# Attention and quantised FFN in one kernel: key rows split over ScalarE and GpSimd, weight maxima earlier, quantising moved around

## The chip, the cores and the metric

The kernel runs on one core of a Trainium2 chip. The metric is the device time of one execution in microseconds (us). Three runs of the kernel before gave 394.27, 394.17 and 396.25; their median is 394.27 us.

## What is computed

Eight sequences of 512 tokens with 512 channels pass through one gated cross-attention block and one gated feed-forward block. The attention is over channels, not tokens: in each of 4 heads a 128 x 128 score matrix is built from 512 tokens, once with a set of global weights and once with local ones. The feed-forward block quantises its inputs and weights to integers with one scale for a whole tensor, so that a maximum over everything has to be known before the first product.

```python
def _channel_attention(qm, km, vm, scale):            # 4 heads
    scores = einsum('bhdn,bhen->bhde', qh, kh) * scale
    attn = softmax(scores, axis=-1)
    return einsum('bhde,bhen->bhdn', attn, vh)
att = attention(q*wqg+bqg, k*wkg+bkg, v*wvg+bvg) + attention(q*wql+bql, k*wkl+bkl, v*wvl+bvl)
x = x + tanh(g_xattn) * (2.0 * att * wp + bp)         # q = layernorm(x), k = v = ctx
def _qlinear(x2d, w, b):
    xq, sx = x/scale rounded, scale = max(max|x|, 1e-6)/127      # one scale per tensor
    wq, sw = the same of w
    return (xq @ wq.T + b) * (sw * sx)
x = x + tanh(g_ffn) * _qlinear(gelu(_qlinear(layernorm(x), w1, b1)), w2, b2)   # 512 -> 2048 -> 512
```

## The kernel before, in words

There is no scheduler: each engine's program is written out by hand, and semaphores join them. Three stages follow each other.

**Attention, steps b = -1 to 7.** A step works on two batches: it finishes batch b and begins batch b+1. Step by step, in the order in which TensorE takes them:
- `gram(b+1)` (L917): products of normalised queries and keys, four heads, 16 matmuls of 129 columns.
- `turn_weights(b)` (L948): transposes of the normalised exponentials. ScalarE's `weights_out` (L433) copies them out of PSUM.
- `key_sums(b+1)` (L925) and `turn_columns` (L930): small products that give the bias terms of the scores.
- `constant_sums(b)` (L958).
- `rank_terms(b+1)` (L937): the bias terms of the scores as a product of two narrow tiles. Its left side is `L_sb` (ScalarE, L440), its right side are the **key rows** `Rh`: (psK + a column) times a constant tile, on 64 partitions (VectorE, `key_rows`, L586).
- `value_product(b)`: a constant row (L969, it needs VectorE's `constant_row`, L650) and the product with the transposed context (L975, it needs `value_weights`, L657).

VectorE's order in step b (2 to 5): `statistics(b+2)` (L556, L560), `columns` (L568), `products` (L577, two), one piece of `w1_max` (L615), `largest_square(b-1)` (L600), `key_rows(b+1)` (L586), `constant_row(b)` (L650), `value_weights(b)` (L657), `scores(b+1)` (L594, eight), `add_product(b)` (L664, four), with `reciprocals` (L635) ahead of its last tile. ScalarE: `weights_out`, `left_rows`, `local_out` (L446), `normalise(b+2)` (L454), `exponentials(b+1)` (L463), `squares(b)` (L425). GpSimd: `rstd_x(b+2)` (L322 to L327), `key_sum(b+2)` (L334, L337), `rstd_out(b-1)` (L351, L357), `weighted(b+1)` (L342, L345: exponentials times their reciprocal sums).

Beside this the first weight matrix is loaded in four quarters `load_w1(0..3)` (L237), each with a semaphore of its own (`w1_in0` to `w1_in3`). `w1_max` reduces it in 16 pieces, four to a quarter. Before, pieces 0 to 3 are taken in step 0, 4 to 8 in steps 1 to 5, 9 to 15 in step 6, where the scale of w1 is made (L694 to L624, with a transpose on TensorE, L907). GpSimd then quantises w1 in eight pieces (L364 and L366 each): five in step 6, three in step 7, and each releases a load of w2. In step 6 VectorE, not GpSimd, weights batch 7's exponentials (L643). The loads of SyncE are issued in the order of its program; `load_k(b)` waits for `gram(b-2)`, `load_cT(b)` for `value_product(b-2)`.

**The scale of x.** After the last attention step VectorE forms the largest normalised value: L727, L732, L735, L737, a transpose on TensorE, L740; GpSimd takes the root (L388), after its own last `rstd_out` (L357); VectorE makes the scale and its reciprocal (L743 to L749) and quantises batch 0 tile by tile (L771, L766), TensorE transposes each tile (L1031), VectorE copies them (L787).

**The two products of the feed-forward block** (L1069 with gelu on ScalarE, L513; L1100 with L851). Hidden values of five batches are spilled to memory and read back.

## Time and profile before

| | |
|---|---|
| median of 3 runs | 394.27 us (394.17 to 396.25) |
| the profiled execution | 394.15 us, its span 392.3 us |
| PE (TensorE matmul) busy | 365.2 us, 93% |
| DVE (VectorE) busy | 320.3 us, 82% |
| ACT (ScalarE) busy | 259.2 us, 66% |
| POOL (GpSimd) busy | 105.5 us, 27% |
| chain that ended last, by engine | PE 80%, DVE 13%, issue 3%, DMA 2%, ACT 1%, POOL 1% |
| attention, from the first product L917 to the last L975 | 13.9 to 143.4 us |
| first FFN product L1069, second L1100 | from 155.0, from 277.7 us |

Times in the profile count from the span's start. The busy shares are averages over stages with different limits. The chain of waits goes back from the last instruction to what released each piece of work; a piece's time in it is only what lies on the chain. A granted clock of 1.00 is TensorE at 2.4 GHz, 0.50 is 1.2 GHz. PEld is TensorE's weight load, SPq the queue of SyncE.

### The profile page before, as it was taken

How to read it: one execution, taken by the hardware profiler on the slowest of the kernel's cores; microseconds unless marked ns; L12 is line 12 of the kernel's file. 1: busy time of each engine (PE TensorE's matmuls, PEld its weight loads, DVE VectorE, ACT ScalarE, POOL GpSimd, SP SyncE). 2: the span in 40 equal slices, each digit the busy share in tenths (PEclk: the TensorE clock that was granted, in tenths of full speed). 3: DMA queues.
4: the chain of work that ended last, by engine and by line, in shares of the span. 5: the costliest groups of instructions: out<-in, count | busy, mean ns of one | idle time of the engine just before them, and what ended most of it. 6: DMA issues, size and time to landing. Idle time of an engine off the chain costs nothing.

```text
span 392.3 us, 5890 instructions
## 1 busy us (share of the span) xinstructions
PE 365.2 (93%) x2087; PEld 218.0 (56%) x2110; DVE 320.3 (82%) x599; ACT 259.2 (66%) x474; POOL 105.5 (27%) x169
## 2 busy tenths in 40 slices
PE   6779899999997797999999999999999999999995
PEld 4657787687685675454455455455544444444442
DVE  3289999999999877999999989978598876686653
ACT  1578877877874450789959988788899997620000
POOL 2653855855845661039200000000000000000000
PEclk9699999999999698999999999999999999999999
DMA  7999987843232550467767760000499999920123
GB/s 223 321 376 382 388 304 281 270 176 100 100 109 67 201 162 3 186 254 297 301 248 305 304 250 0 3 0 2 179 390 402 424 427 423 340 119 28 81 109 107
DMA packets 14528, 84.74 MB, mean 216 GB/s; under 512 B 1889, under 2 KB 2145, under 8 KB 5026
## 3 DMA queue, kind: packets, MB, share of 16 engines
q1 hardware_dynamic: 13840, 83.89, 56.3%
q10 hardware_dynamic: 658, 0.46, 0.5%
q8 instruction: 17, 0.28, 0.3%
q14 instruction: 13, 0.11, 0.1%
HBM read 54.99 MB, written 29.36 MB: 215 GB/s over the span
## 4 chain that ended last, share of the span: by engine, by line
PE 80%; DVE 13%; issue 3%; DMA 2%; ACT 1%; POOL 1%; DVEq 0%; SPq 0%; POOLq 0%
PE PS L1069 28%; PE PS L1100 28%; PE PS L975 7%; PE PS L917 7%; DVE mxd L600 3%; PE PS L937 2%; PE PS L969 2%; PE PS L1031 2%; DVE mid L577 2%; DMA X<-in_x 2%; DVE ring L643 1%; PE PS L958 1%; DVE mid L586 1%; DVE hmax L615 1%; PE PS L948 1%
## 5 line engine op out<-in xcount | busy, mean ns | idle before, releaser
L513 ACT ACTIVATE ring<-PS,bias,sc 128x512 f32<-128x512 f32 x128 | 97.1, 782 | 30.3 <-PE PS L1069 17.3
L1069 PE MATMUL PS<-mid,w1q 128*128 128x512 bf16 x500 | 111.9, 382 | 1.8 <-DVE mid L787 1.3
L1100 PE MATMUL PS<-w2q,w1q 128*128 128x512 bf16 x501 | 110.0, 379 | 1.1 <-DVE w1q L869 0.6
L1100 PEld LDWEIGHTS PS<-w2q,w1q 128*128 128x128 bf16 x512 | 49.9, 98 | 60.9 <-issue 0.5
L1069 PEld LDWEIGHTS PS<-mid,w1q 128*128 128x128 bf16 x512 | 50.0, 98 | 60.7 <-issue 2.6
L800 DVE TENSOR_REDUCE hmax<-ring 128x1 f32<-128x2048 f32 x30 | 67.5, 2278 | 5.4 <-ACT ring L513 5.4
L532 ACT ACTIVATE ring<-ring,sc 128x2048 f32<-128x2048 f32 x30 | 57.6, 1990 | 7.2 <-DMA ring<-spilled_hidden 7.2
L860 DVE TENSOR_SCALAR w1q<-ring 128x2048 bf16<-128x2048 f32 x30 | 36.6, 1223 | 22.8 <-PE PS L1100 18.7
L917 PE MATMUL PS<-ring 128*128 128x129 f32 x256 | 32.0, 286 | 1.4 <-ACT ring L454 1.4
L975 PEld LDWEIGHTS PS<-w2q,ring 128*128 128x128 f32 x256 | 29.2, 192 | 6.1 <-issue 6.1
L917 PEld LDWEIGHTS PS<-ring 128*128 128x128 f32 x256 | 31.2, 202 | 1.7 <-issue 1.7
L975 PE MATMUL PS<-w2q,ring 128*128 128x128 f32 x256 | 30.7, 278 | 0.0
L463 ACT ACTIVATE ring<-mid,nb 128x128 f32<-128x128 f32 x64 | 24.7, 388 | 8.3 <-DVE nb L594 8.3
L556 DVE BATCH_NORM_STATS2 st<-X 128x6 f32<-128x512 f32 x32 | 19.9, 681 | 11.9 <-issue 6.1
L851 DVE SCALAR_TENSOR_TENSOR X<-PS,sc,X 128x512 f32<-128x512 f32 (+1 forms) x33 | 22.9, 730 | 8.1 <-PE PS L1100 7.1
L664 DVE SCALAR_TENSOR_TENSOR X<-PS,X 128x512 f32<-128x512 f32 x32 | 21.8, 688 | 4.8 <-PE PS L975 4.4
L454 ACT ACTIVATE ring<-X,nmr,rstd 128x512 f32<-128x512 f32 x32 | 23.4, 811 | 3.2 <-POOL nmr L327 3.2
L903 PE MATMUL PS<-ident 128*128 128x128 f32 x124 | 19.7, 314 | 5.3 <-POOL ident L310 3.5
L425 ACT ACTIVATE ring<-X,nmean 128x512 f32<-128x512 f32 x32 | 22.8, 714 | 0.5
L903 PEld LDWEIGHTS PS<-ident 128*128 128x128 f32 x124 | 17.7, 221 | 8.0 <-POOL ident L310 3.5
L879 DVE TENSOR_TENSOR X<-X,mid 128x1024 f32<-128x1024 f32 x16 | 19.4, 1218 | 0.0
L337 POOL TENSOR_TENSOR mid<-mid,ring 128x512 f32<-128x512 f32 x16 | 18.9, 1184 | 1.3
(108 smaller groups left out, 405.6 us busy)
## 6 DMA issues: line engine op xcount, KB each, us to landing
spilled_hidden<-ring SPq DMA_DIRECT2D x20, 1024.0 KB, 3.9
ring<-spilled_hidden SPq DMA_DIRECT2D x20, 1024.0 KB, 8.9
ring<-in_ctx SPq DMA_DIRECT2D x8, 1024.0 KB, 10.0
ring<-in_ctxT SPq DMA_DIRECT2D x8, 1024.0 KB, 5.3
X<-in_x SPq DMA_DIRECT2D x7, 1024.0 KB, 12.8
out<-X SPq DMA_DIRECT2D x7, 1024.0 KB, 10.5
ring<-in_w1T SPq DMA_DIRECT2D x4, 1024.0 KB, 10.4
ring<-in_w2T SPq DMA_DIRECT2D x8, 512.0 KB, 3.8
```

The costliest lines, as they stand in the source:

```text
L454: nc.scalar.activation(q_sb[b % 2][:, i].rearrange("p h d -> p (h d)"), X[:, b, i, :], ACT.Identity, scale=rstd1[:, i:i + 1], bias=nmr1[:, ...
L463: nc.scalar.activation(E_sb[:, j, :], S_sb[:, j, :], ACT.Exp, scale=-1.0, bias=nb[:, j:j + 1], accum_out=Z[:, j:j + 1]).then_inc(exp_done, 1)
L513: nc.scalar.activation(ring[:, s * CH + c, (h % CH) * N:(h % CH + 1) * N], PS[:, hidden_bank(s, h), :], ACT.Gelu, scale=S1, bias=bias1[:, ...
L532: nc.scalar.activation(r, r, ACT.Copy, scale=ISH, bias=MAGIC).then_inc(hy_done, KH // CH)
L800: V.tensor_reduce(hmax[:, bass.ds(CH * g + c, 1)], ring[:, s * CH + c, :], AX.X, ALU.max, apply_absolute_value=True).then_inc(hm_done, 1)
L851: V.scalar_tensor_tensor(xi, PS[:, par * NT + i, a:a + n], S2, xi, ALU.mult, ALU.add).then_inc(out_done, 1)
L860: V.tensor_scalar(hq[:, c].rearrange("p k n -> p (k n)"), ring[:, s * CH + c, :], MAGIC, None, ALU.subtract).then_inc(hq_done, KH // CH)
L903: nc.tensor.matmul(PS[:, bank, 0:P], ident[:, :], ident[:, :], start=True, stop=True)
L917: mm = nc.tensor.matmul(psG[:, h // 2, h % 2, :], q_sb[b % 2][:, i, h, :], k_sb[b % 2][:, i, h, :], start=(i == 0), stop=(i == NT - 1))
L975: mm = nc.tensor.matmul(PS[:, OUT_BANK[i], h * P:(h + 1) * P], cT_sb[b % 2][:, h, i, :], M_sb[b % 2][:, h, :], start=False, stop=(h == NH ...
L1069: mm = nc.tensor.matmul(PS[:, hidden_bank(s, h), :], w1v[:, k, h * P:(h + 1) * P], xqT[:, s, k, :], start=(k == 0), stop=(k == NH - 1))
L1100: mm = nc.tensor.matmul(PS[:, par * NT + i, :], hq[:, c, k, i * P:(i + 1) * P], w2v[:, kk, :], start=(kk == 0), stop=(kk == KH - 1))
```

## The change

- **Key rows** of batches 2 to 7: ScalarE copies psK out of PSUM with the column added (`key_copy`, behind `weights_out`), and GpSimd multiplies by the constant tile (`key_rows`, behind `rstd_x`). Batches 0 and 1 stay on VectorE.
- **Weight maxima**: pieces 0 to 2 before step -1, 3 in step -1, 4 to 7 in step 0, b+7 in step b (1 to 5), 13 to 15 in step 6. `load_w1(0)` and `load_w1(1)` are issued three loads earlier.
- **GpSimd** quantises pieces 0 and 1 of w1, then waits until batch 7's exponentials are weighted (`en_done`), and then does pieces 2 to 4 (and 5 to 7 as before).
- **The scale of x**: the root gives the inverse at once, so one reciprocal and one product leave the path; they and the bias go to `x_scale`, behind the first quantising.
- **Batch 0's quantising**: tiles 1 and 3 are scaled by ScalarE, 0 and 2 by VectorE.
- **Warm-up matmuls** before the first product: 11 where there were 2.

```diff
@@ -247,14 +248,14 @@
...
             load_x(1)
+            load_w1(0)
             load_k(1)
...
             load_cT(0)
-            load_w1(0)
+            load_w1(1)
             load_k(2)
...
             load_cT(1)
-            load_w1(1)
             for b in range(2, B):
@@ -305,7 +306,6 @@
...
                 nc.gpsimd.memset(k_sb[s][:, :, :, P:HEAD], 1.0).then_inc(consts, 1)
-            nc.gpsimd.memset(PHALF, 0.5)
             pool.wait_ge(zeroed, 3)
@@ -335,6 +335,11 @@
...
+            def key_rows(b):
+                pool.wait_ge(kc_done, b - 1)
+                nc.gpsimd.tensor_tensor(Rh[0:64, :], Rh[0:64, :], rowc[0:64, :], ALU.mult).then_inc(rh_done, 1)
@@ -369,11 +374,17 @@
...
                     rstd_x(b + 2)
+                if 1 <= b < B - 1:
+                    key_rows(b + 1)
+                if b + 2 < B:
                     key_sum(b + 2)
-                if b >= 1 and b < B:
+                if 1 <= b < B:
                     rstd_out(b - 1)
                 if b == B - 2:
-                    for q in range(5):
+                    quantise_w1(0)
+                    quantise_w1(1)
+                    pool.wait_ge(en_done, 8 * B)
+                    for q in range(2, 5):
                         quantise_w1(q)
@@ -385,7 +396,7 @@
...
             pool.wait_ge(xs_step, 4)
-            nc.gpsimd.tensor_tensor(XROOT, XALL, PHALF, ALU.pow).then_inc(xs_pow, 1)
+            nc.gpsimd.tensor_tensor(XROOT, XALL, half[:, 0:1], ALU.pow).then_inc(xs_pow, 1)
@@ -432,6 +443,12 @@
...
+            def key_copy(b):
+                act.wait_ge(sk_done, b + 1)
+                act.wait_ge(r_done, b)
+                nc.scalar.activation(Rh[0:64, :], psK, ACT.Identity, scale=1.0, bias=acol[0:64, 64:65]).then_inc(kc_done, 1)
@@ -480,6 +497,8 @@
...
                 weights_out(b)
+                if 1 <= b < B - 1:
+                    key_copy(b + 1)
                 if b + 1 < B:
@@ -496,6 +515,10 @@
...
             act.wait_ge(t_done, B)
+            act.wait_ge(xs_step, 7)
+            for i in (1, 3):
+                nc.scalar.activation(ring[:, 3, i * D:(i + 1) * D], X[:, 0, i, :], ACT.Identity,
+                                     scale=rstd[:, i:i + 1], bias=nmr1[:, i:i + 1]).then_inc(ya_done, 1)
             act.wait_ge(scales, 1)
@@ -677,27 +700,29 @@
...
             statistics(1)
+            w1_max(range(0, 3))
             dve.wait_ge(blocks_in, 32)
...
                 if b == B - 2:
-                    w1_max(range(9, 13))
+                    w1_max(range(13, 16))
                 if b + 1 < B:
...
                 if 1 <= b < B - 2:
-                    w1_max([b + 3])
+                    w1_max([b + 7])
                 if b == B - 2:
-                    w1_max(range(13, 16))
                     dve.wait_ge(w1_step, 4 * NH)
...
                     largest_square(b - 1)
-                if b + 1 < B:
-                    key_rows(b + 1)
+                if b == -1:
+                    key_rows(0)
+                    w1_max([3])
                 if b == 0:
-                    w1_max(range(0, 2))
+                    key_rows(1)
+                    w1_max(range(4, 6))
                 if b == B - 2:
@@ -715,7 +740,7 @@
...
                 if b == 0:
-                    w1_max(range(2, 4))
+                    w1_max(range(6, 8))
                 if b >= 0:
@@ -740,14 +765,19 @@
...
             dve.wait_ge(rstd_done, B)
-            V.tensor_scalar(SX, XROOT, MIN_RANGE, 1.0 / QP, ALU.max, ALU.mult).then_inc(xs_step, 1)
+            V.tensor_scalar(ISX, XROOT, QP, QP / MIN_RANGE, ALU.mult, ALU.min).then_inc(xs_step, 1)
             dve.wait_ge(xs_step, 5)
-            V.reciprocal(ISX, SX).then_inc(xs_step, 1)
-            V.tensor_tensor(S1, SX, SW1, ALU.mult).then_inc(xs_step, 1)
-            dve.wait_ge(xs_step, 7)
             V.tensor_scalar(rstd[:, :], rstd[:, :], ISX, None, ALU.mult).then_inc(xs_step, 1)
-            V.tensor_scalar(bias1[:, :], B1, S1, None, ALU.mult).then_inc(scales, 1)
+            dve.wait_ge(xs_step, 6)
+            V.tensor_tensor(nmr1[:, :], nmean[:, 0:NT], rstd[:, 0:NT], ALU.mult).then_inc(xs_step, 1)
+            def x_scale():
+                V.reciprocal(SX, ISX).then_inc(xs_step, 1)
+                dve.wait_ge(xs_step, 8)
+                V.tensor_tensor(S1, SX, SW1, ALU.mult).then_inc(xs_step, 1)
+                dve.wait_ge(xs_step, 9)
+                V.tensor_scalar(bias1[:, :], B1, S1, None, ALU.mult).then_inc(scales, 1)
@@ -758,24 +788,32 @@
...
                     dve.wait_ge(hm_done, CH * (g - SLOTS + 1) + 1)
-                dve.wait_ge(xs_step, 8)
+                dve.wait_ge(xs_step, 6)
                 yt = ring[:, s * CH + 3, :].rearrange("p (i d) -> p i d", i=NT)
                 xq = ring[:, s * CH + 2, 0:CW // 2].bitcast(BF16)
+                first = isinstance(g, int) and g == 0
+                def normal(i, inc):
+                    V.tensor_scalar(yt[:, i, :], X[:, g, i, :],
+                                    nmean[:, bass.ds(4 * g + i, 1)], rstd[:, bass.ds(4 * g + i, 1)],
+                                    ALU.add, ALU.mult).then_inc(y_done, inc)
                 def to_integers(i):
-                    dve.wait_ge(y_done, 4 * g + i + 1)
+                    if i % 2 == 0:
+                        dve.wait_ge(y_done, i + 2)
+                    else:
+                        dve.wait_ge(ya_done, (i + 1) // 2)
                     V.tensor_scalar(xq[:, i * D:(i + 1) * D], yt[:, i, :], MAGIC, MAGIC, ALU.add,
...
-                first = isinstance(g, int) and g == 0
-                for i in range(NT):
-                    V.tensor_scalar(yt[:, i, :], X[:, g, i, :],
-                                    nmean[:, bass.ds(4 * g + i, 1)], rstd[:, bass.ds(4 * g + i, 1)],
-                                    ALU.add, ALU.mult).then_inc(y_done, 1)
-                    if first and i > 0:
-                        to_integers(i - 1)
                 if first:
-                    to_integers(NT - 1)
+                    normal(0, 2)
+                    normal(2, 2)
+                    for i in range(NT):
+                        to_integers(i)
                 else:
+                    for i in range(NT):
+                        normal(i, 1)
                     dve.wait_ge(y_done, 4 * g + 4)
@@ -801,6 +839,7 @@
...
             quantise_x(0, 0, 0)
+            x_scale()
             evacuate(0, 0)
@@ -983,10 +1022,12 @@
...
             mm.then_inc(spread_done, 1)
+            keep_warm(2, 6)
             pe.wait_ge(nmr_done, 1)
-            keep_warm(1, 6)
-            pe.wait_ge(q_done, 1)
-            keep_warm(1, 6)
+            keep_warm(3, 6)
+            for i in range(NT - 1):
+                pe.wait_ge(q_done, i + 1)
+                keep_warm(2, 6)
             pe.wait_ge(consts, 9)
@@ -1046,7 +1087,7 @@
...
             keep_warm(4)
-            pe.wait_ge(xs_step, 8)
+            pe.wait_ge(xs_step, 6)
             keep_warm(3)
...
             pe.wait_ge(w1q_done, PIECES)
```

**VectorE, step 1.** Before (the left name is the tile written, `hmax` holds the maxima, `mxd` the largest squares; `w1_in1` and `w1_in2` are the semaphores of w1's second and third quarter):

```order
L568 TENSOR_TENSOR acol<-PS,colv 128x2x4 [waits aT_done,g_done]
L577 TENSOR_TENSOR mid<-PS,w2q 128x512 [waits exp_done]
L577 TENSOR_TENSOR mid<-PS,w2q 128x512
L615 TENSOR_REDUCE hmax<-ring 128x1 [waits w1_in1]
L600 TENSOR_REDUCE mxd<-ring 128x4 [waits sq_done]
L586 SCALAR_TENSOR_TENSOR mid<-PS,acol,mid 64x512 [waits r_done,sk_done]
L650 TENSOR_TENSOR ring<-PS,mid 128x512 [waits o_done,c_done,scaled]
```

Now:

```order
L591 TENSOR_TENSOR acol<-PS,colv 128x2x4 [waits aT_done,g_done]
L600 TENSOR_TENSOR mid<-PS,w2q 128x512 [waits exp_done]
L600 TENSOR_TENSOR mid<-PS,w2q 128x512
L638 TENSOR_REDUCE hmax<-ring 128x1 [waits w1_in2]
L623 TENSOR_REDUCE mxd<-ring 128x4 [waits sq_done]
L673 TENSOR_TENSOR ring<-PS,mid 128x512 [waits o_done,c_done,scaled]
```

The key rows have left VectorE's queue, and the maximum in it waits for another quarter of w1.

**SyncE, the first loads.** Before, and then now (`in_ctx` are the keys, `in_ctxT` the transposed context):

```order
L228 DMA ring<-in_ctx 128x16x128
L222 DMA X<-in_x 128x2048
L228 DMA ring<-in_ctx 128x16x128
L222 DMA X<-in_x 128x2048
L234 DMA ring<-in_ctxT 128x2048
L237 DMA ring<-in_w1T 128x2048
L228 DMA ring<-in_ctx 128x16x128 [waits g_done,ks_step]
L222 DMA X<-in_x 128x2048
L234 DMA ring<-in_ctxT 128x2048
L237 DMA ring<-in_w1T 128x2048
L228 DMA ring<-in_ctx 128x16x128 [waits g_done,ks_step]
```

```order
L229 DMA ring<-in_ctx 128x16x128
L223 DMA X<-in_x 128x2048
L238 DMA ring<-in_w1T 128x2048
L229 DMA ring<-in_ctx 128x16x128
L223 DMA X<-in_x 128x2048
L235 DMA ring<-in_ctxT 128x2048
L238 DMA ring<-in_w1T 128x2048
L229 DMA ring<-in_ctx 128x16x128 [waits g_done,ks_step]
L223 DMA X<-in_x 128x2048
L235 DMA ring<-in_ctxT 128x2048
L229 DMA ring<-in_ctx 128x16x128 [waits g_done,ks_step]
```

The first and the second quarter of w1 stand three loads earlier; behind the last row the order is the same in both, with the third quarter three loads on.

**GpSimd, step 6.** Now (`sc` holds the scale of w1; before, five pairs like the first stood here with no wait on `en_done`, and no row `kc_done`):

```order
L342 TENSOR_TENSOR mid<-mid 64x512 [waits kc_done]
L356 TENSOR_SCALAR ve<-ssq 128x4 [waits sq_done]
L362 TENSOR_TENSOR rstd<-ve,half 128x4 [waits ve_done]
L369 TENSOR_SCALAR ring<-ring,sc 128x1024 [waits w1_step]
L371 TENSOR_SCALAR w1q<-ring 128x1024 [waits w1y_done]
L369 TENSOR_SCALAR ring<-ring,sc 128x1024 [waits w1_step]
L371 TENSOR_SCALAR w1q<-ring 128x1024 [waits w1y_done]
L369 TENSOR_SCALAR ring<-ring,sc 128x1024 [waits w1_step,en_done]
L371 TENSOR_SCALAR w1q<-ring 128x1024 [waits w1y_done]
```

The third pair now waits until batch 7's exponentials are weighted.

## Rows read from the trace of the kernel before

**Rows 1.** Chain of waits, step 2: start, us on the chain, what

```profile
57.30 0.17 DVE acol L568
...
58.66 0.59 DVE hmax L615
59.26 2.16 DVE mxd L600
61.41 0.70 DVE mid L586
...
62.25 1.09 PE PS L937 x3
...
71.61 0.17 DVE acol L568
```

**Rows 2.** Timeline, step 2: start, us, engine, line, operation, tiles, count

```profile
58.07 1.07 PE L925 MATMUL PS<-mid,ring 128*64 128x512 f32 x2
58.18 1.09 ACT L433 ACTIVATE w2q<-PS 128x512 f32<-128x512 f32 x2 [0.46 <-PE PS L948]
...
59.31 2.05 PE L958 MATMUL PS<-w2q 128*128 128x128 f32 x16
```

**Rows 3.** Groups by line and shape: busy us, mean ns, idle before

```profile
L454 ACT ACTIVATE ring<-X,nmr,rstd 128x512 f32<-128x512 f32 x32 | 23.4, 811 | 3.2 <-POOL nmr L327 3.2
...
L337 POOL TENSOR_TENSOR mid<-mid,ring 128x512 f32<-128x512 f32 x16 | 18.9, 1184 | 1.3
```

**Rows 4.** One line (L237) in the window 39 to 40 us: third quarter of w1

```profile
L237 SPq DMA_DIRECT2D ring<-in_w1T x1: 433/433/433, 39.4 to 39.4; - x1
...
DMA to landing us min/median/max: 10.2/10.2/10.2
```

**Rows 5.** Windows: length, busy of PE, PEld, DVE, ACT, POOL, clock, DMA share, GB/s

```profile
14.00:35.00 21.00, 18.96 (x114) 13.83 (x114) 15.95 (x57) 14.39 (x43) 12.44 (x16) 0.91 1.01 378
35.00:49.00 14.00, 12.88 (x105) 10.96 (x103) 14.00 (x46) 11.84 (x37) 8.35 (x17) 1.00 1.01 372
```

**Rows 6.** Timeline, step 1, VectorE

```profile
44.27 0.67 DVE L615 TENSOR_REDUCE hmax<-ring 128x1 f32<-128x512 f32 x1
...
47.72 0.67 DVE L650 TENSOR_TENSOR ring<-PS,mid 128x512 f32<-128x512 f32 x1
```

**Rows 7.** Windows around the two late low stretches of the clock

```profile
136.50:140.00 3.50, 2.66 (x18) 1.71 (x17) 1.28 (x2) 0.00 (x0) 3.42 (x4) 0.86 0.01 2
...
156.80:160.00 3.20, 3.20 (x14) 1.33 (x13) 3.09 (x3) 2.26 (x4) 0.00 (x0) 0.82 0.00 0
```

**Rows 8.** Chain of waits, from step 6 to the first FFN product

```profile
122.05 1.14 PE PS L969 x8
...
127.16 4.79 DVE ring L643 x8
...
137.79 0.70 DVE ring L650
...
146.55 0.09 DVE ve L727
...
148.69 0.56 POOL sc L388
...
152.20 0.46 DVE ring L771
...
155.03 8.29 PE PS L1069 x31
```

**Rows 9.** Timeline of the fill, VectorE

```profile
15.17 2.47 DVE L556 BATCH_NORM_STATS2 st<-X 128x6 f32<-128x512 f32 x4 [6.09 <-issue]
...
27.87 1.67 DVE L643 TENSOR_SCALAR ring<-ring,rw 128x128 f32<-128x128 f32 x8
```

**Rows 10.** Timeline, GpSimd, the first two of eight pieces of w1

```profile
121.41 1.13 POOL L364 TENSOR_SCALAR ring<-ring,sc 128x1024 f32<-128x1024 f32 x1 [5.08 <-DVE sc L624]
...
123.65 1.13 POOL L364 TENSOR_SCALAR ring<-ring,sc 128x1024 f32<-128x1024 f32 x1
```

More of the change, by code:

```diff
@@ L85, in gated_xattn_ffn @@
         (W1MAX, W1ALL, SW1, ISW1, W2MAX, W2ALL, SW2, ISW2, XMAX, XALL, XROOT, SX, ISX, S1,
-         HMAX, HALL, SH, ISH, S2, PHALF) = (sc[:, i:i + 1] for i in range(20))
+         HMAX, HALL, SH, ISH, S2) = (sc[:, i:i + 1] for i in range(19))
         w1max, w2max4 = hmax[:, 0:4 * NH], hmax[:, 4 * NH:4 * NH + CH]
@@ L170, in gated_xattn_ffn @@
             ("q_done", "ks_step", "g_done", "sk_done", "rh_done"))
+        kc_done, ya_done = sem("kc_done"), sem("ya_done")
         a_done, aT_done, L_done, r_done = (sem(n) for n in ("a_done", "aT_done", "L_done", "r_done"))
```

## The prediction

> **What bounds the kernel now.** I read the page first: TensorE is busy 93% of the span and the chain that ended last is TensorE for 80%, so a gain has to come from where TensorE waits. Then the chain of waits in order of time. The two 8-batch matmul phases behind 155 us (L1069, L1100) run without gaps that the diff touches, so they are left as they are. What the diff touches lies in the first 155 us, and there the chain leaves TensorE once per attention step. The reader is to see this in [rows 1], step b=2: one piece of weight maximum (0.59), the largest square (2.16) and the key rows (0.70) stand in VectorE's queue one behind the other, and only then do the rank terms L937 run, at 62.25. TensorE had ended its last work, L958, at 59.31+2.05=61.36 [rows 2]. A step lasts 71.61-57.30=14.31 us, and the chain repeats these rows for b=2 to 5.
>
> **Steps 2 to 5: the key rows leave VectorE.** The key sums L925 end at 58.07+1.07=59.14, and ScalarE's weights_out L433 at 58.18+1.09=59.27 [rows 2]. The new key_copy stands right behind it. Its price isn't in the trace; between one of the two L433 (1.09/2=0.55) and L454, which has two pointer operands and reads SBUF (0.81), I take 0.65, nearer the first, since it reads PSUM too: it ends near 59.95. The Trainium skill, "ScalarE: Activation LUTs", section What ACT_TABLE_LOAD costs, gives 280 ns + 0.833 ns an element for a pointer bias, an estimate of 0.71 us, by which the key rows would come 0.05 before TensorE is free, and the sum would be the same. GpSimd's product of SBUF tensors is priced by L337, 1.18 [rows 3]; half the partitions don't shorten it in this pricing. Key rows are ready near 61.25, not 62.10, and TensorE is free at 61.36: the rank terms start 0.89 earlier, and VectorE reaches the constant row 0.7 earlier too. Two things give a little back. ScalarE arrives 0.65 later at the exponentials, so VectorE's reciprocal has to wait some 0.35, part of which its slack before the next columns takes. And GpSimd's key sum starts behind its product, hidden, since GpSimd is busy 8.35 of 14 us [rows 5]. I take 0.8 a step: **-3.2 us** over four (bounds 0, if the copy and product come 0.9 later, and -3.6).
>
> **Step 1: a new wait.** The maxima are moved ahead: step 1 now reduces piece 8, not piece 4. Piece 8 is the first of the third quarter of w1 (order: w1_in1 becomes w1_in2). That load is not moved. It is issued at 39.4 and lands 10.2 us later, at 49.65 [rows 4]. It can't come sooner: the DMA engines are busy 1.01 of their share from 14 to 49 us, at 372 to 378 GB/s [rows 5], and the megabytes ahead of it are the same ones in another order. VectorE reaches the piece at 44.27 [rows 6]. So it stands still for 5.3 us, and queued behind it are the largest square, the constant row, the value weights and the scores. From 49.7, 0.59+2.16 put the constant row L650 at 52.45, where it had started at 47.72 [rows 6]: 4.7 later. TensorE has done its rank terms by 48 and waits for that row; without them beside it, L969 (1.14 alone, as in [rows 8]) is through some 0.3 sooner. That is **+4.4 us** (bounds +3.4 and +5.4, if the load lands a us away).
>
> TensorE then has had nothing for over 5 us. No row shows such a gap in a warm stretch, but two low stretches of the granted clock lie behind sparser ones. The window from 136.5 has 0.86, so half clock (1.2 GHz) lasted until about 137.5, while work had been steady since L643 ended at 131.95 [rows 8]; the window from 156.8 has 0.82, low until about 157.95, with L1069 steady from 155.03 [rows 7, 8]. So 2.9 to 5.5 us of steady work ran at half clock, and half of that is lost: 1.45 to 2.75. I take **+2.0 us** (lower bound 0, no drop). The skill's "TensorE: Matmul & The Clock Gate", section Terms, reckons the same way (time throttled times one minus K/N); it would give 1.5 for 3 us and 2.0 for 4.
>
> **The fill.** w1's first quarter now stands third in the queue. VectorE's statistics of the second batch begin with its landing at 15.17 [rows 9]; a megabyte at 378 GB/s [rows 5] is 2.8 us later, near 18, just as they end. Three pieces at 0.6 bring the first columns to 19.8, where they were. The loads of key rows, inputs and transposed context between move back by a megabyte, 2.8 us, and by my reading each is used over a us after that. The nine extra warm-up matmuls run while ScalarE normalises; in case the clock is low they could delay the first products by 1 us, but VectorE isn't back from its maxima by then. I take 0 (bounds -0.3, +1).
>
> **Step 6.** Three maxima and a reduction less in front of the largest square, and no key rows. Before, L969 started at 122.05 [rows 8]. Now the scale of w1 waits for TensorE (L958, then the transpose): near 119.05; the scale 0.6, the constant row 0.7: L969 at 120.4. **-1.6 us.** Then VectorE's weighting L643: 4.79 for 8 beside GpSimd's quantising [rows 8], but 1.67 for 8 in the fill with GpSimd nearly idle [rows 9]. GpSimd now does two pieces at 2.24 [rows 10], from 119.7 to 124.2, and stops; the weighting starts at 125.5. **-3.1 us.** Behind it the constant row started 5.85 us after the weighting ended (131.94 to 137.79), in the low clock of [rows 7]. Warm, L948 0.4, weights_out 1.1 and L958 2.05 with their gaps make 3.9: **-1.9 us** (bounds 0 and -2).
>
> **What is late next: GpSimd.** It takes up piece 2 at 127.15. Six pieces at 2.24, rstd_out(6) at 1.3, and it is free at 141.9 for the last rstd_out (1.0) and then the root L388: 143.0. VectorE's ve L727 would come at 139.9 (146.55 less 6.6) and the root was 2.14 us behind it before [rows 8], so it could have been at 142.0: **+1.0 us.** Up to the root: 148.69 to 143.05, -5.6.
>
> **The first quantising.** Tiles 1 and 3 on ScalarE take two passes of 0.46 [rows 8] out of VectorE's chain, and a reciprocal and a product leave it. ScalarE's two passes at 0.81 run beside tiles 0 and 2; tile 3 ends near 1.65 us after the start, when VectorE is at integer tile 3 anyway: **-1.2 us** (bounds 0 and -1.5). x_scale's three small operations go before the evacuation, while TensorE transposes.
>
> **Sum.** -3.2 +4.4 +2.0 +0 -1.6 -3.1 -1.9 +1.0 -1.2 = **-3.6**. The profiled execution took 394.15 (span 392.3), 0.12 below the median of the runs, 394.27. So 390.5 us. What a measurement here can tell from no change is about 0.5%, or 2 us: under 392.3 is faster, over 396.2 slower.
>
> **Rivals.**
> - *No stall in step 1* (0.07): the third quarter lands by 44.3, or the wait doesn't stand on it. Then step 1 gains the 1.07 of its key rows instead: 394.15-10.0-1.1 = 383.0. For it: no row; against it [rows 4, 5].
> - *The gains up front are not had* (0.15): copy and product together need 0.5 us more than I take, since only 0.1 us lies between them and TensorE; the exponentials, later by as much, then hold VectorE. The gain of 0.8 a step shrinks to 0.2, +2.4, and GpSimd's late root, if its pieces run at 2.4 beside VectorE, adds 1: 393.9, no difference.
> - *Slower* (0.06): the clock, once fallen in the gap at 48 to 53 us, stays at 1.2 GHz. It is one mechanism; each us of TensorE work at half clock costs half a us. It decides the sign when 5.7 us more than my 2.0 are lost, thus when the low stretch holds 15.5 us of work, more than a whole step. If it lasts through the next step, with its 13 us of TensorE work (12.88 in 14, [rows 5]), the loss is 13 more: 403.6. Against it: low stretches ended 2.9 to 5.5 us after work was steady [rows 7].
> - *As forecast* (0.72): its own range is 388.0 to 392.8, from the clock (0 to +2.75), the landing (a us) and the steps' gain.
>
> **How the numbers follow.** The forecast is the likeliest case, 390.5. The range 387.0 to 393.9 takes it with its bounds and the second rival, and leaves out the first and third and the tails. Faster by over 0.5%: most of the forecast case (0.69), the first rival (0.07): 0.76. Within: the second rival and the forecast's upper end, 0.18. Slower: 0.06.
>
> **What would show it.** Right: in the waits, VectorE's maximum waits 5 us for the load of w1, near 44 to 50 us; TensorE idles before L969 of step 1; the granted clock of 50 to 58 us is under 1; steps 2 to 5 last 13.5 us, not 14.3; the weighting of batch 7 takes 1.7 us; the chain passes over GpSimd's last pieces before the root. Wrong: no DMA wait there, then the first rival; steps that still last 14.3, with TensorE waiting for GpSimd's product, then the second; a weighting that still takes over 3 us, then the -3.1 is false.

## The result and the profile after

The changed kernel takes **390.28 us**, median of 4 runs (389.17 to 390.8), against 394.38 us (394.17 to 396.25) for the kernel before in 4 runs: ratio 0.9882, 95% interval 0.9844 to 0.992. That is faster by over 0.5%, 4.1 us, against 3.6 forecast. The profiled execution is the fastest of the four, 389.17 us with a span of 387.4, so profile against profile the gain is 4.9 us of span. The other three have a mean granted clock of 0.985, the profiled one 0.991. Line numbers below are those of the changed kernel: L964 is `key_sums` (L925 before), L976 `rank_terms`, L1008 the constant row's product (L969), L1014 the product with the transposed context (L975).

The page, busy time of each engine (share of the span) and the chain's shares:

```profile
PE 367.0 (95%) x2105; PEld 217.1 (56%) x2128; DVE 312.6 (81%) x592; ACT 263.0 (68%) x482; POOL 112.3 (29%) x174
...
PE 72%; DVE 16%; POOL 4%; issue 3%; DMA 2%; ACT 1%; DVEq 0%; POOLq 0%; SPq 0%; ACTq 0%
```

**Step 1** in the chain of waits (start, us, what), where [rows 6] stood before:

```profile
40.41 8.85 DMA ring<-in_w1T
...
49.28 0.07 DVE hmax L638
...
49.88 2.28 DVE mxd L623
52.16 0.61 DVE ring L673
...
52.81 2.09 PE PS L1008 x8
54.90 4.92 PE PS L1014 x32
59.82 3.57 PE PS L956 x32
```

The third quarter of w1 is on the chain: VectorE reaches its maximum L638 and stands there until the load lands at 49.26. The waits of this stretch (engine, line, what it waits for; us in total, times, longest) say the same, and show who stands behind it:

```profile
PEld PS L1008 <- DVE ring L673: 4.8, 1, 4.8
...
DVE hmax L638 <- DMA ring<-in_w1T: 4.0, 1, 4.0
PE PS L1008 <- DVE ring L673: 3.9, 1, 3.9
ACT ring L480 <- DVE nb L617: 3.9, 1, 3.9
```

The windows (length, busy of PE, PEld, DVE, ACT, POOL, granted clock, DMA share, GB/s) show what the gap did to TensorE, and that the late low stretches of [rows 7] are gone in this execution:

```profile
48.00:52.00 4.00, 0.88 (x4) 0.05 (x2) 2.72 (x2) 2.26 (x4) 3.68 (x5) 0.81 0.99 313
52.00:56.00 4.00, 3.19 (x13) 1.69 (x14) 3.45 (x22) 1.89 (x10) 0.73 (x1) 0.50 0.34 141
56.00:60.00 4.00, 4.00 (x33) 4.00 (x32) 2.35 (x8) 1.30 (x8) 0.14 (x1) 0.84 0.00 0
...
136.00:140.00 4.00, 4.00 (x38) 4.00 (x37) 2.98 (x9) 2.73 (x9) 3.75 (x6) 1.00 0.67 231
156.80:160.00 3.20, 3.15 (x27) 1.97 (x27) 3.20 (x2) 2.12 (x3) 0.00 (x0) 1.00 0.70 287
```

From 52 to 56 us TensorE has 1.2 GHz: L1008 takes 2.09 instead of 1.14, L1014 4.92 instead of 3.78 (both in [rows 8] or the chain behind them).

**The key rows** stand in the timeline as ScalarE's copy and GpSimd's product:

```profile
45.58 0.68 ACT L451 ACTIVATE mid<-PS,acol 64x512 f32<-64x512 f32 x1
...
46.34 1.26 POOL L342 TENSOR_TENSOR mid<-mid 64x512 f32<-64x512 f32 x1 [0.32 <-ACT mid L451]
```

0.68 was taken as 0.65, 1.26 as 1.18. The key sums start at 64.20, 77.65, 91.09, 104.54 and 117.99: a step is 13.45 us, against 14.31 before, and VectorE is no longer on the chain between the key sums and the rank terms.

**Step 6 to the second product**, chain of waits:

```profile
122.85 1.14 PE PS L1008 x8
...
127.95 1.67 DVE ring L666 x8
...
129.71 1.13 POOL ring L369
...
130.91 1.04 POOL w1q L371
...
144.43 1.01 POOL rstd L362
145.45 0.53 POOL sc L399
146.00 0.16 DVE sc L768
...
146.58 1.00 DVE ring L797 x2
147.58 1.34 DVE ring L806 x4
...
150.70 1.83 DVE ring L797 x4
...
152.63 1.23 DVE ring L818
153.86 6.58 DVE hmax L651 x3
```

The weighting (L666) takes 1.67, not the 4.79 of [rows 8]. From 129.7 GpSimd is the chain: six pieces of w1 and two `rstd_out` end at 145.45, where the root starts without waiting for VectorE. And behind the quantising VectorE, not TensorE, holds the start of the feed-forward block; before, [rows 8] had TensorE's L1069 there.

Where the span's 4.9 us come from, both profiles read at the same events (starts of the key sums, of the constant row's product, of the weighting, of the root, of the second product):

| stretch | before | after | moved | forecast |
|---|---|---|---|---|
| start to the key sums behind step 1 | 58.07 | 64.20 | +6.13 | +6.4 (0, +4.4, +2.0) |
| four steps | 57.24 | 53.79 | -3.45 | -3.2 |
| key sums to L1008 of step 6 | 6.74 | 4.86 | -1.88 | -1.6 |
| L1008 to the weighting's end | 9.90 | 6.77 | -3.13 | -3.1 |
| weighting's end to L1008 of step 7 | 6.58 | 4.55 | -2.03 | -1.9 |
| L1008 of step 7 to the root | 10.16 | 11.28 | +1.12 | +1.0 |
| root to the second product | 129.03 | 127.20 | -1.83 | -1.2 |
| second product to the end | 114.6 | 114.7 | +0.1 | 0 |

### The profile page after: what moved, and what is told of

It is laid out like the page before. It is cut to its first block, busy times and chain, and to the rows that moved or that the text cites. A ratio compares the mean times of both kernels' runs of the same rounds, so it can differ in the third digit from the quotient of the medians.

```text
span 387.4 us, 5934 instructions
## 1 busy us (share of the span) xinstructions
PE 367.0 (95%) x2105; PEld 217.1 (56%) x2128; DVE 312.6 (81%) x592; ACT 263.0 (68%) x482; POOL 112.3 (29%) x174
## 4 chain that ended last, share of the span: by engine, by line
PE 72%; DVE 16%; POOL 4%; issue 3%; DMA 2%; ACT 1%; DVEq 0%; POOLq 0%; SPq 0%; ACTq 0%
PE PS L1141 28%; PE PS L1110 16%; PE PS L1014 7%; DVE hmax L838 6%; PE PS L956 6%; PE PS L997 3%; DMA ring<-in_w1T 2%; DVE hmax L651 2%; PE PS L942 2%; PE PS L976 2%; PE PS L1008 2%; POOL ring L369 2%; DVE ring L797 2%; POOL w1q L371 2%; PE PS L964 2%
## 5 line engine op out<-in xcount | busy, mean ns | idle before, releaser
L1014 PEld LDWEIGHTS PS<-w2q,ring 128*128 128x128 f32 x256 | 30.3, 198 | 6.9 <-issue 6.9
L1014 PE MATMUL PS<-w2q,ring 128*128 128x128 f32 x256 | 31.7, 284 | 0.0
L956 PE MATMUL PS<-ring 128*128 128x129 f32 x256 | 29.9, 275 | 0.0
L956 PEld LDWEIGHTS PS<-ring 128*128 128x128 f32 x256 | 29.2, 192 | 0.0
L942 PE MATMUL PS<-ident 128*128 128x128 f32 x142 | 22.1, 315 | 5.2 <-POOL ident L310 3.5
L942 PEld LDWEIGHTS PS<-ident 128*128 128x128 f32 x142 | 20.4, 225 | 8.3 <-POOL ident L310 3.5
L918 DVE TENSOR_TENSOR X<-X,mid 128x1024 f32<-128x1024 f32 x16 | 19.4, 1218 | 0.0
```

Source lines behind the costliest of these rows:

```text
L942: nc.tensor.matmul(PS[:, bank, 0:P], ident[:, :], ident[:, :], start=True, stop=True)
L956: mm = nc.tensor.matmul(psG[:, h // 2, h % 2, :], q_sb[b % 2][:, i, h, :], k_sb[b % 2][:, i, h, :], start=(i == 0), stop=(i == NT - 1))
L1014: mm = nc.tensor.matmul(PS[:, OUT_BANK[i], h * P:(h + 1) * P], cT_sb[b % 2][:, h, i, :], M_sb[b % 2][:, h, :], start=False, stop=(h == NH ...
```

## The experiments

My theory was the sum as forecast: four gains of together some 10 us, and one load that takes 6 back in step 1. The rivals: the stall is not the load's, the gains come from elsewhere than the parts that I named, and TensorE's clock is not the gap's doing. Times are medians; the kernel before took 394.54, 394.44 and 394.77 us in the three groups of runs (x1 to x4, x5 to x8, x9 to x12). Ratios are to it.

### x1: the stall taken away

```
-                if 1 <= b < B - 2:
-                    w1_max([b + 7])
+                if 2 <= b < B - 2:
+                    w1_max([b + 6])
                 if b == B - 2:
-                    w1_max(range(13, 16))
+                    w1_max(range(12, 16))
```

> The changed kernel, but step 1 reduces no piece of w1: pieces 8 to 11 come in steps 2 to 5 and four pieces instead of three in step 6. Theory (the maximum of piece 8 waits for a load that lands at 49.3 us, and TensorE's clock falls in the gap): the wait of 3.96 us goes, and with it the 1.2 us that L1008 and 1.1 us that L1014 took longer in the low clock; step 1 then lasts as the steps behind it, L1014 of step 1 starts near 49.8 instead of 54.9; 384.0 us, 6.3 under the changed kernel's 390.3. Rival (the loads as a whole are the bound up to step 3, so that the next load stops VectorE or TensorE instead): under 2 us gained, and a DMA wait in step 2 or 3.

Measured: 382.36 us (381.54 to 382.74), ratio 0.9692 (0.9655 to 0.9729). That is 1.6 under what was expected. Span 380.9: 6.5 under the changed kernel's, as expected. The medians are 7.9 apart, since the profiled execution of the changed kernel is its fastest, 1.1 us under its median; what made the others longer no profile shows. Its chain in step 1 is TensorE alone:

```profile
47.54 1.11 PE PS L976 x4
48.65 0.87 PE PS L1008 x6
49.52 3.79 PE PS L1014 x32
```

and the granted clock is 1.00 from 48 to 60 us. Step 1 now lasts 13.45 us like the others (44.25 to 57.70). The whole stall and the low clock came from one maximum that stands one step too early. No other version here has a lower median; x6, x9 and x11 lie within 0.8 us of it and can't be told from it.

### x2: the gap filled with dummy products, the stall kept

```
+                if b == 1:
+                    keep_warm(15, 6)
                 if b == -1:
                     pe.wait_ge(s_done, 2)
```

> The changed kernel with its wait, and 15 warm-up matmuls on TensorE in the gap of step 1, behind the rank terms. Theory (the low clock behind the gap is a cost of its own): the granted clock of 52 to 56 us is 1.00, L1008 takes 1.14 instead of 2.09 and L1014 3.8 instead of 4.9, 388.2 us, 2.1 less than the changed kernel. Rival (the low clock would be hidden by VectorE's or ScalarE's work of that step): within 0.5 us of the changed kernel.

Measured: 387.14 us (387.0 to 389.22), ratio 0.9828 (0.9785 to 0.9871). The chain and, under it, the clock's window:

```profile
39.03 10.14 DMA ring<-in_w1T
...
52.73 1.14 PE PS L1008 x8
53.87 3.79 PE PS L1014 x32
```

```profile
52.00:56.00 4.00, 3.27 (x27) 2.48 (x28) 4.00 (x25) 1.97 (x11) 0.00 (x0) 1.00 0.32 131
```

L1008 starts where it did (52.73 and 52.81), and L956 at 57.67 instead of 59.82: the clock alone costs **2.15 us**, and with the gap filled it doesn't fall. In the medians x2 is 3.1 us under the changed kernel, 2.1 in the spans. The load landed at 49.17 and 49.26 in the two profiles (here and in the changed kernel) though the first key sums of their fills are 2.3 us apart (18.30 and 20.58), so the wait is 5.3 here and 4.0 there: VectorE comes sooner and stands longer. The dummies (30 matmuls in the trace, 3.62 us) don't fill the whole of it: TensorE still idles 1.67 us before L1008, instead of 3.94, and the clock holds.

### x3: the key rows back on VectorE (on top of x1)

```
@@ GpSimd
-                if 1 <= b < B - 1:
-                    key_rows(b + 1)
@@ ScalarE
-                if 1 <= b < B - 1:
-                    key_copy(b + 1)
@@ VectorE
+                if 1 <= b < B - 1:
+                    key_rows(b + 1)
```

> Like x1_no_stall, with the key rows of all batches back on VectorE as before the change. Theory (the key rows stand on the path of every step): steps 2 to 5 last 14.3 us instead of 13.45, step 1 loses 1.0, step 6 next to nothing as the scale of w1 waits for TensorE there: 4.5 us more than x1_no_stall, 388.5. Rival (moving the rows only shifts the wait to GpSimd's product or to ScalarE, and the shorter steps come from the maxima): under 1.5 us more than x1_no_stall.

Measured: 386.36 us (386.22 to 387.97), ratio 0.9805 (0.9765 to 0.9845), 4.0 over x1. Steps 2 to 5 are 14.31 long again, by this chain:

```profile
72.77 0.59 DVE hmax L634
73.36 2.16 DVE mxd L619
75.51 0.70 DVE mid L605
...
76.35 1.09 PE PS L974 x3
```

A piece of the maximum, the largest square and the key rows stand in one queue ahead of the rank terms, as in [rows 1]. The split of the key rows is worth 0.86 us a step, and TensorE works through a step once they are gone from VectorE.

### x4: the maxima moved, nothing else (on the kernel before)

```
             load_x(1)
+            load_w1(0)
...
             load_cT(0)
-            load_w1(0)
+            load_w1(1)
...
+            w1_max(range(0, 3))
...
-                    w1_max(range(9, 13))
+                    w1_max(range(13, 16))
...
-                    w1_max([b + 3])
+                    w1_max([b + 7])
```

The three maxima at the end of step 6 go, piece 3 is taken in step -1 and pieces 4 to 7 in step 0, as in the change.

> The kernel before with one part of the change alone: the order of the loads of w1 and of its maxima, pieces 0 to 2 in the fill, b+7 in step b, three in step 6. Theory (that part holds the stall): step 1 waits 5 us for the third quarter of w1 as in the changed kernel, 4.9 us and 2.0 for the clock are lost, 1.8 us in step 6 and little else are won: 399 us, slower than before by 1.2%. Rival (the stall exists only because the other parts make step 1 come sooner): no wait and 392 to 394 us.

Measured: 400.03 us (397.97 to 401.0), ratio 1.0125 (1.0073 to 1.0177). Alone, this part of the change is **slower**. Its windows:

```profile
48.00:52.00 4.00, 0.00 (x0) 0.00 (x0) 1.92 (x2) 1.42 (x3) 2.41 (x4) 1.00 0.99 287
52.00:56.00 4.00, 2.24 (x10) 1.73 (x12) 3.37 (x8) 0.00 (x0) 0.00 (x0) 0.50 0.48 199
56.00:60.00 4.00, 4.00 (x18) 2.53 (x13) 2.04 (x17) 3.18 (x16) 0.00 (x0) 0.50 0.00 0
```

With the key rows still behind the waiting maximum, the rank terms wait too (6.5 us), TensorE has nothing at all from 48 to 52, and the clock stays at 0.50 from 52.0 to 62.3 us. The key sums behind step 1 come at 67.95, 9.9 late. The weighting takes 4.77 here: its gain isn't the maxima's.

### x5: without GpSimd's pause around the weighting (on top of x1)

```
-                    pool.wait_ge(en_done, 8 * B)
```

> Like x1_no_stall (382.4 us), but GpSimd doesn't wait for the weighting of batch 7: it quantises pieces 0 to 4 of w1 in a row, as before the change. Theory (the contended weighting costs 3.1 us and lets TensorE's clock fall, 1.9 us, against 1.0 that the late root costs): the weighting L666 takes 4.8 us for 8 instead of 1.67, the clock is at half near 125 to 132 us, the root comes 4.0 us later after the start of step 6's L1014: 386.4 us. Rival (what the weighting gains is given back by GpSimd's pieces, which then stand on the chain): within 1 us of x1_no_stall.

Measured: 386.55 us (386.06 to 387.25), ratio 0.9804 (0.9775 to 0.9832), 4.1 to 4.2 over x1. Chain, and the window behind it:

```profile
121.51 4.88 DVE ring L665 x8
...
132.08 0.70 DVE ring L672
...
143.05 0.56 POOL sc L398
```

```profile
126.00:130.00 4.00, 3.57 (x17) 3.58 (x18) 3.79 (x11) 2.81 (x8) 1.19 (x2) 0.50 0.74 245
```

x1 has the weighting at 121.44 with 1.66 and the root at 138.98. One wait on GpSimd does it all. VectorE's eight small scalings take 4.88 us beside GpSimd's pieces and 1.66 without them. With the wait, TensorE is busy 3.72 of the 4 us from 122 to 126 (1.55 in x5), its clock does not fall to 0.50, and GpSimd, which gives up 3 us of work, comes only 1 us late to the root. The single instructions in the trace of x5 show what the sharing looks like: four of the eight scalings take 1.06 to 1.16 us, and each of these ends 0.08 us behind the end of a GpSimd instruction; the other four take 0.27 to 0.28, as they do in x1.

### x6: the fill's dummy products as before (on top of x1)

```
-            keep_warm(2, 6)
             pe.wait_ge(nmr_done, 1)
-            keep_warm(3, 6)
-            for i in range(NT - 1):
-                pe.wait_ge(q_done, i + 1)
-                keep_warm(2, 6)
+            keep_warm(1, 6)
+            pe.wait_ge(q_done, 1)
+            keep_warm(1, 6)
```

> Like x1_no_stall, with 2 warm-up matmuls in front of the first products L956 as before the change, instead of 11. Theory (the nine more stand in TensorE's queue and hold the first products until 16.8 us where the clock is low): the first products begin at 13.9, and the first columns at 19.8 instead of 20.6 us; 0.5 to 1 us less. Rival A (VectorE's three maxima hold the columns in any case): no change. Rival B (the warm-ups buy the clock, without them the products run at half clock, 5.7 instead of 3.6 us, and end as late): no change or up to 0.5 us more.

Measured: 382.98 us (382.15 to 384.34), ratio 0.9712 (0.9681 to 0.9744): no difference to x1 that these runs can tell. Rival A held: the first columns start at 19.53 here, behind VectorE's three maxima, and at the same time with the extra dummies where the fill is quick (19.39 in x2, 19.42 in x9).

The fill itself comes in two kinds. In the profiles of the changed kernel, x1, x5, x7 and x11 the six products of L1023, which stand ahead of the extra dummies in TensorE's program, take 5.5 us; in all the others they take 2.8 to 3.2. Here is that line of the timeline for the changed kernel and for x2:

```profile
7.18 5.48 PE L1023 MATMUL PS<-ring 1*128 1x512 f32 x6
```

```profile
7.19 3.02 PE L1023 MATMUL PS<-ring 1*128 1x512 f32 x6
```

The first key sums start at 20.58 and 20.34 in the one case, 18.30 and 17.97 in the other, 19.35 in x6. The windows print a granted clock of 1.00 for the slow fill, but that is no reading: the trace's clock records begin at 15.5 to 18.8 us in the five slow profiles and at 6.4 to 7.9 in the others, each time with 1.00, and a window without a record is printed as 1.00. By their length, nearly twice the 2.8 to 3.2, the products of the slow fill ran at 1.2 GHz; that is argued from the length, since no record covers them.

Of the 2.37 us between x1 and x9 the second key sums (30.68 and 30.03) show only 0.65, and the root 0.69. The maxima hold x9's first columns until 19.42, where x1's start at 20.52, and then x9's clock is at 0.50 from 24.0 to 27.4 us, where x1's stays at 1.00: the second L956 is on x9's chain with 5.21 us. In x2, with the quick fill and no such fall, the second key sums come at 29.55.

### x7: all four first tiles on VectorE (on top of x1)

```
-            for i in (1, 3):
-                nc.scalar.activation(ring[:, 3, i * D:(i + 1) * D], X[:, 0, i, :], ACT.Identity, ...
```

and VectorE's loop of scaling and rounding as before.

> Like x1_no_stall, with all four tiles of batch 0 scaled on VectorE, tile by tile, as before the change; the scale of x keeps its new form. Theory (two passes of 0.46 us stand on the path to the first FFN product): 0.9 us between the scale and the copies L825, 0.7 to 0.9 us more in all, 383.2. Rival (the first group of the FFN is held by VectorE's maxima behind it and hides it): no change.

Measured: 385.33 us (383.14 to 387.05, 6 runs), ratio 0.9773 (0.9738 to 0.9807): 2.1 more than I had expected. From the root's end to the first product it takes 5.37 instead of 4.48, the 0.9 of the tiles. But then:

```profile
146.00:150.00 4.00, 3.35 (x8) 1.12 (x9) 3.89 (x7) 0.78 (x1) 0.00 (x0) 0.50 0.02 4
150.00:154.00 4.00, 4.00 (x16) 1.62 (x14) 4.00 (x3) 2.56 (x4) 0.00 (x0) 0.76 0.00 0
```

TensorE comes out of its waits for the tiles at 1.2 GHz, and the first 32 products take 9.67 us.

### x8: GpSimd's last piece of w1 behind the root (on top of x1)

```
-                    for q in range(5, PIECES):
+                    for q in range(5, PIECES - 1):
...
+            quantise_w1(PIECES - 1)
```

> Like x1_no_stall, but GpSimd quantises its last piece of w1 behind the root L399, not in front of its last rstd_out. Theory (GpSimd is late for the root by 1.07 us): the root comes 1.1 us sooner and its last piece ends 2.2 us behind it, before TensorE's first FFN product: 381.3 us. Rival (the piece then shares the time of VectorE's scalings of batch 0 and slows them, or TensorE waits for it): no gain or up to 1 us more.

Measured: 383.78 us (383.25 to 384.25), ratio 0.9732 (0.9704 to 0.9761): a miss, 1.4 more than x1 instead of 1.1 less. The root does come 1.0 sooner, counted from the last but one value product (118.00 to 138.46; in x1 117.42 to 138.94), but the chain goes on so:

```profile
138.49 0.56 POOL sc L399
...
139.26 0.93 DVE rstd L771
...
140.33 1.69 DVE ring L798 x2
```

GpSimd's piece now runs from 139.02 beside VectorE's scaling: 0.93 instead of 0.25, and 1.69 instead of 1.00. The 0.93 end at 140.18, 0.03 us behind GpSimd's first instruction. 1.0 won, 1.4 lost.

### x9 to x12: what the clock at the start of the feed-forward block is worth

x7 and x8 had left open how much of their time was a clock that fell around the quantising. x9 is x1 once more; x10, x11 and x12 are x1, x8 and x7 with

```
             pe.wait_ge(xs_step, 6)
-            keep_warm(3)
+            keep_warm(7)
             transposes(0, 0)
+            keep_warm(6)
```

> The kernel of the first experiment once more (the changed kernel, with the maxima of w1 one step later), beside the three that follow, since its time and theirs came from different jobs. If nothing but noise lies between jobs: 382.4 us, between 381.5 and 383. If its first time was a lucky phase of the clock: up to 384.5, with a granted clock under 1.00 somewhere between 138 and 150 us.

> The same with 7 dummy products instead of 3 ahead of the first transposes and 6 more behind them, in the holes of 0.6 and 1.1 us that TensorE has there. Theory (the clock at the start of the FFN falls in some executions because TensorE idles around the quantising): the granted clock stays 1.00 from 138 to 160 us in the profile, and the median is that of the kernel without them or up to 1 us under it, with less spread between executions: 381.5 to 382.5. Rival (VectorE holds the start of the FFN anyway, so that TensorE's clock there is worth nothing): no change, 382.4; or the dummies delay the first product: +0.2 to +0.9.

> GpSimd's last piece of w1 behind the root, as in x8, with the same dummy products. In x8 the root came 1.07 us sooner but the granted clock fell to 0.80 and 0.78 between 142 and 150 us and the first 32 products took 8.6 us. Theory (the clock took the gain): clock 1.00 and 381.5 to 382.3, 1.5 to 2 us under x8. Rival (GpSimd's piece beside VectorE's scaling is what costs, and VectorE sets the start): 383 to 384 in spite of a clock of 1.00.

> All four tiles of the first group scaled by VectorE, as before the change, with the same dummy products. x7, without them, took 385.3 us, 2.9 more than x1, where the longer quantising (3.96 instead of 3.44 us) explains 0.5. Theory (the clock at the start of the FFN took the rest: 0.50 from 146 to 150 us there): with the dummies 383 to 383.5. Rival (something else in the move of the two tiles, or the late fill of 1.4 us in that profile): stays above 384.5.

| | us | ratio (95%) | clock 142 to 146, 146 to 150 | first product | root to second product |
|---|---|---|---|---|---|
| x1 | 382.36 | 0.9692 (0.9655 to 0.9729) | 1.00, 1.00 | 143.99 | 127.2 |
| x9 | 382.82 | 0.970 (0.9683 to 0.9716) | 0.68, 0.89 | 143.30 | 128.0 |
| x10 | 383.8 | 0.9717 (0.9693 to 0.9741) | 1.00, 1.00 | 143.90 | 127.2 |
| x8 | 383.78 | 0.9732 (0.9704 to 0.9761) | 0.80, 0.78 | 144.69 | 129.0 |
| x11 | 383.08 | 0.970 (0.9679 to 0.9721) | 1.00, 1.00 | 144.67 | 128.6 |
| x7 | 385.33 | 0.9773 (0.9738 to 0.9807) | 0.89, 0.50 | 146.66 | 129.7 |
| x12 | 383.62 | 0.9716 (0.9697 to 0.9736) | 1.00, 1.00 | 144.59 | 128.1 |

x1 and x9 are one kernel: in one profile the clock holds, in the other it falls,

```profile
142.00:146.00 4.00, 2.91 (x11) 1.06 (x10) 3.86 (x9) 0.78 (x1) 0.00 (x0) 0.68 0.01 4
```

and the medians differ by 0.46 us. With the dummies it held in all three profiles. That they did it is likely but not shown: of the nine profiles with the new scale of x and without these dummies, five hold the clock there as well (the changed kernel, x1, x2, x3, x5), and four fall (x6 to x9). From the root to the second product that is worth 0.8 us (x9 against x10) where the clock falls briefly, 1.6 (x7 against x12) where it falls deep. It isn't more, because VectorE is close behind: its reductions of the hidden values are the chain there when TensorE is fast. In the medians x12 is 1.7 under x7, as in this stretch of the profiles, so the clock is likely the larger part of the 2.1 that x7 took over what was expected; but x7's profile also has the slow fill, with its first columns at 22.0 instead of 19.4, and how often that came in its other runs isn't known. x11 is 0.7 under x8 and no faster than x9: with a good clock the earlier root still gives its microsecond back to the contention. x10, which should have been the fastest, is not: two of its four runs took 384.2 and 384.3 at a mean clock of 0.993, and I have no profile of these. That stays open. Two tiles on ScalarE are 0.9 us in the profiles (127.2 and 128.1) and nothing in the medians of x10 and x12.

## Why the prediction was right, by its steps

- **Steps 2 to 5** (-3.2): -3.45, 0.86 each. Copy and product cost 0.1 more together than taken and still fit in, and x3 took 4.0 us back when they were undone, as its profile adds up: 0.5 in step 1 and 0.86 in four. The rival of gains not had is out. Of the 0.09 a step that I took off for the late exponentials only 0.03 were lost: TensorE has no gap in the step any more. The copy took 0.68, between my 0.65 and the 0.71 that I had estimated from the Trainium skill's "ScalarE: Activation LUTs", What ACT_TABLE_LOAD costs.
- **Step 1** (+4.4, clock +2.0): +6.13 in all. x2 splits it: with the clock held, the key sums behind step 1 come at 62.04, so the load is +4.0 and the clock +2.15. The landing was forecast from the unchanged issue at 49.65 and came at 49.26; the clock's price, read from two low stretches elsewhere, was off by 0.15. x1 and x2 show the cause. By the reckoning of the Trainium skill's "TensorE: Matmul & The Clock Gate", Terms, the 4.5 us at half clock in which TensorE worked (52.8 to 57.3) would cost 2.25; the runs have 2.15. The whole low stretch of the trace, from 50.5, would give 3.4 by it, too much, since in its first part TensorE was idle anyway.
- **The fill** (0): in the profile 0.96 late, as the upper bound allowed, and it cost nothing. What I did not see: the wait for the load in step 1 swallows whatever the fill loses, since the landing doesn't move.
- **Step 6** (-1.6, -3.1, -1.9): -1.88, -3.13, -2.03. The first is the maxima's alone: from the key sums to the constant row's product x4, with nothing but the maxima moved, takes 4.86 like the changed kernel, and so does x3 with its key rows back on VectorE. x5 ties the last two to one wait on GpSimd: 4.1 us at the root (143.05 and 138.98).
- **Late root** (+1.0): +1.12, with GpSimd on the chain from 129.7 as forecast.
- **First quantising** (-1.2): up to the evacuation -1.1 (146.00 to 149.41, before 149.28 to 153.81), up to the second product -1.83. The term itself was right; what the sum lacks is a term for the clock behind it. The low clock that [rows 7] show at 156.8 is gone in the profile of after, and I had used that row only to price step 1, not asked whether a shorter quantising would remove it. By x9 and x10 such a fall is worth about 0.8. Since x1's kernel falls there in x9, it need not be gone in every execution of the changed kernel either; that would be one reason why the median gained 4.1 and the profile 4.9, but no profile shows it.
- **The sum**: 390.5 against 390.28 is closer than the forecast deserves. The stages of the two profiles add up to -4.97, 1.4 more gain than the -3.6; the median lies 1.1 over the profiled execution and takes most of that back. The mechanism was right in each term, the last 0.2 us are luck.
- **No stall**, the first rival, was priced at 383.0; the kernel without the stall, x1, takes 382.4. The mechanism was right though not the case at hand. **Slower**, a clock that stays low, did not happen; nearest to it came x4, where the clock stood at 0.50 for 10.2 us (52.0 to 62.3) and the kernel was 1.25% slower; there too it came back, 8.5 us into the work behind the gap.

## What to carry to other kernels

Before a consumer is moved ahead, look at when its operand lands: here one maximum, a step too early, stood 4 to 5 us on a load in a saturated queue. It cost 6.5 of the 11.4 us that the change takes off the span without it, because TensorE and ScalarE waited 3.9 us each behind it and TensorE's clock fell as well. Where two engines run short passes at each other's cost, a pause of the one that has slack is worth trying: one wait gave 4 us. Work put off on one engine may only move its contention with another: the earlier root of x8 gained 1.0 and lost 1.4.

## What the runs showed that I had not expected

- A printed granted clock of 1.00 can mean that nothing was recorded. In the slow fill, L1023 takes 5.48 us for 6 products in windows printed as 1.00, before the first clock record; in the executions with the quick fill the same windows show the low clock, 0.57 to 0.66 from 10 to 14 us, because they are recorded, and the first products end some 2 us sooner. The mean granted clock counts the unrecorded time as full, so it doesn't rank executions: x11's run at 1.00 took 383.09, its run at 0.995 took 382.11. Judge the clock at the start by the length of known instructions.
- The contention between VectorE and GpSimd is no fixed factor: 1.00 to 1.69 for two scalings of 128x512 (x8), 1.66 to 4.88 for eight of 128x128 (x5), and 0.25 to 0.93 for one of 128x32. In x5 and in the last of these the lengthened pass ends 0.03 to 0.08 us behind a GpSimd instruction of 1.0 to 1.2 us, so a short pass pays in proportion more.
- A gap of 3.9 us in the middle of steady work brought TensorE to 1.2 GHz until about 57.3 us, 4.5 us into the work behind it; and around the quantising, with gaps of 0.6 to 1.1 us only, the same kernel fell in one profile (x9) and not in another (x1).
